# Who begins the 16 transfers that turn a state's last chunk into rows: SyncE and ScalarE, or SyncE alone

## What is computed

```python
for _ in range(5):
    a_in  = Af @ (state @ in_W.T + in_b)
    a_out = Af.T @ (state @ out_W.T + out_b)
    a = concat([a_in, a_out, state])
    r = sigmoid(a @ r_W.T + r_b);  z = sigmoid(a @ z_W.T + z_b)
    h_hat = tanh(concat([a_in, a_out, r * state]) @ h_W.T + h_b)
    state = (1 - z) * state + z * h_hat
out = layernorm(x + tanh(state @ o1_W.T + o1_b) @ o2_W.T + o2_b)
```

## Time and profile before

| | before |
|---|---|
| median of 3 runs | 664.33 us (664.10 to 664.61) |
| the profiled execution | 664.52 us |
| its span in the trace | 662.7 us |
| TensorE busy | 649.4 us, 98% |
| VectorE busy | 476.7 us, 72% |
| ScalarE busy | 409.9 us, 62% |
| GpSimd busy | 50.7 us, 8% |
| mean granted TensorE clock | 0.996 of full speed |

### The profile page before, as it was taken

The page is one execution under the profiler, slowest core; times in us unless marked ns, Lnnn a source line. Parts: engine busy times, 40 slices in busy tenths (PEclk is TensorE's granted clock), DMA queues, the critical chain, the costliest instruction groups (busy, mean ns, idle before and its releaser), DMA issues.

```text
span 662.7 us, 8655 instructions
## 1 busy us (share of the span) xinstructions
PE 649.4 (98%) x2940; PEld 538.7 (81%) x2940; DVE 476.7 (72%) x774; ACT 409.9 (62%) x550; POOL 50.7 (8%) x49
## 2 busy tenths in 40 slices
PE   8999999999999999999999999999999999999993
PEld 7888888888888888888888888888888888888883
DVE  4986878697487759847784994687489658725886
ACT  2873735479456837864593688368458935763646
POOL 0074034200400000000000000000000000000002
PEclk9999999999999999999999999999999999999998
DMA  8996533213000130300003022000322200013003
GB/s 286 311 407 241 169 130 106 42 42 52 3 0 32 51 47 32 52 13 0 32 33 62 0 64 32 0 32 32 50 46 60 35 1 1 1 64 127 1 1 130
DMA packets 90515, 46.72 MB, mean 70 GB/s; under 512 B 72176, under 2 KB 78960, under 8 KB 90224
## 3 DMA queue, kind: packets, MB, share of 16 engines
q1 hardware_dynamic: 86128, 45.77, 24.0%
q10 hardware_dynamic: 4352, 0.53, 0.5%
HBM read 32.12 MB, written 11.53 MB: 66 GB/s over the span
## 4 chain that ended last, share of the span: by engine, by line
PE 93%; DVE 3%; DMA 1%; SPq 1%; ACT 1%; issue 0%; DVEq 0%
PE bank L561 26%; PE bank L548 17%; PE bank L550 17%; PE bank L549 17%; PE bank L612 15%; DMA work<-in_x_dram 1%; DVE stats L1552 1%; DVE a L1545 0%; DVE sums L1524 0%; DVE ring L1139 0%; ACT rows L811 0%; SPq L389 0%; ACT a L1123 0%; SPq L391 0%; DVE work L1585 0%
## 5 line engine op out<-in xcount | busy, mean ns | idle before, releaser
L901 ACT ACTIVATE work<-work,bias 128x512 f32<-128x512 f32 x120 | 86.1, 723 | 155.5 <-DVE work L1280 155.0
L561 PE MATMUL bank<-ring,rows 128*128 128x512 f32 x768 | 178.6, 389 | 0.0
L561 PEld LDWEIGHTS bank<-ring,rows 128*128 128x128 f32 x768 | 144.0, 188 | 30.2 <-ACT ring L811 0.2
L1280 DVE SCALAR_TENSOR_TENSOR work<-degree,deg_w,bank 128x512 f32<-128x512 uint16 x120 | 88.7, 745 | 57.6 <-PE bank L550 56.5
L811 ACT ACTIVATE ring<-a 128x1024 fp32r<-128x1024 uint8 (+1 forms) x115 | 116.4, 1048 | 8.7 <-PE bank L561 6.6
L548 PE MATMUL bank<-u_c,fold 128*128 128x512 f32 x240 | 93.5, 389 | 0.0
L550 PE MATMUL bank<-u_c,fold 128*128 128x512 f32 x240 | 93.4, 389 | 0.0
L549 PE MATMUL bank<-u_c,fold 128*128 128x512 f32 x240 | 93.4, 389 | 0.0
L612 PE MATMUL bank<-ring,rows 128*128 128x512 f32 x256 | 65.0, 391 | 0.0
L548 PE MATMUL bank<-st_c,own 128*128 128x512 f32 x160 | 62.3, 389 | 0.0
L550 PE MATMUL bank<-st_c,own 128*128 128x512 f32 x160 | 62.2, 389 | 0.0
(11 more groups left out here) (147 smaller groups left out, 924.2 us busy)
## 6 DMA issues: line engine op xcount, KB each, us to landing
stage<-in_adj_dram SPq DMA_DIRECT2D x15, 512.0 KB, 8.9
sums<-in_adj_dram SPq DMA_DIRECT2D x13, 512.0 KB, 8.6
turned_dram<-work SPq DMA_DIRECT2D x12, 512.0 KB, 2.6
rows<-turned_dram SPq DMA_DIRECT2D x192, 32.0 KB, 2.0
work<-in_x_dram SPq DMA_DIRECT2D x4, 512.0 KB, 10.6
x_dram<-work SPq DMA_DIRECT2D x4, 512.0 KB, 8.8
a<-x_dram SPq DMA_DIRECT2D x4, 512.0 KB, 5.4
a<-in_adj_dram SPq DMA_DIRECT2D x3, 512.0 KB, 11.1
```

The source lines that it names most:

```text
L561: m = nc.tensor.matmul(u_bank[2 * (c % 2) + d][:, :], rows[:, part, j, d * P:(d + 1) * P], tile[:, jj, :], start=(first and jj == 0 and pa ...
L901: nc.scalar.activation(gates[:, g, e, :], gates[:, g, e, :], ACT.Tanh if g == H else ACT.Sigmoid, bias=bias[:, g, e:e + 1]).then_inc(gate_ ...
L1280: nc.vector.scalar_tensor_tensor(out=gates[:, g, e, :], in0=degree[:, c * CW:(c + 1) * CW], scalar=deg_w[:, g, e:e + 1], in1=g_bank[s % 3] ...
```

## The change

SyncE's `turn_move` runs over all four groups `n` and so begins 16 transfers. ScalarE's `turn_move` and its two calls for each step are gone. Sources, targets, sizes and the semaphore of the transfers stay as they are.

```diff
                 sp.wait_ge(turned, DB * NC * (t + 1))
-                for n in range(NQ - 1):
+                for n in range(NQ):
                     for r in range(NQ):
                         sp.dma_start(rows[n * SQ:(n + 1) * SQ, LO, ...
...
-            def turn_move(t, some):
-
-                k = NC - 1
-                act.wait_ge(turned, DB * NC * (t + 1))
-                for n in range(NQ - 1, NQ):
-                    for r in some:
-                        act.dma_start(rows[n * SQ:(n + 1) * SQ, LO, ...
...
                 for k in range(10, 12):
                     if side == 0:
                         row_high(t, 2, k - 10)
-                        turn_move(t - 1, range(2 * (k - 10), 2 * (k - 9)))
                     cast(t, side, k)
```

More of the change, by code:

```diff
@@ L867, in split_state @@
                 high(st_c[:, HI, e, :], stateT[:, e, c * CW:(c + 1) * CW], st_hi)
-            def turn_move(t, some):
-                k = NC - 1
-                act.wait_ge(turned, DB * NC * (t + 1))
-                for n in range(NQ - 1, NQ):
-                    for r in some:
-                        act.dma_start(rows[n * SQ:(n + 1) * SQ, LO, k * BC:(k + 1) * BC, :].bitcast(F32)
-                                      .rearrange("a b (e r d) -> a (b e) r d", e=DB, r=NQ)[:, :, r, :],
-                                      turned_T[r * SQ:(r + 1) * SQ, n].rearrange("p b e d -> p (b e) d")).then_inc(rows_loaded[k], 16)
             def row_high(t, k, h):
```

## The result

The changed kernel takes 666.91 us (median of 6 runs, 666.42 to 667.97), the kernel before 664.43 us (6 runs, 664.10 to 664.83). The ratio is 1.0038 with a 95% interval of 1.0026 to 1.0050: slower by about 2.5 us. Two more measurements of the same kernel, beside the experiments, gave ratios of 1.0034 (1.0021 to 1.0047) and 1.0033 (1.0021 to 1.0045). The profiled execution took 667.19 us, with a span of 665.4 against 662.7; the mean granted TensorE clock is 0.996 in both. One execution among the experiments, of the kernel with half-size transfers, took 942.8 us at a granted clock of 0.655 and is left out of its ratio.

A forecast was written before the change was run, and what follows sets the result against it. TensorE's own work was taken as the bound. 664.52 + 2.1 + 0.7 = 667.3 us for an execution like the profiled one, 0.2 less for the median: 667.1 us, 8-in-10 range 665.2 to 669.2.

The forecast's parts named there:

- TensorE bounds, nothing else gives: Whole kernel: TensorE is busy 98% of the span; changes elsewhere count only through its stream, and no later idle stretch returns delay.
- ScalarE's relief is worth 0: ScalarE: dropping its 16 issues, some 10 us of issuing, gains 0 because a lead of over 1 us hides them.
- Last issue 9.8 us after the first: SyncE's burst in each step: sixteen issues 0.652 us apart put the last start 9.8 us after the first.
- From the last issue to the row work, 1.98 us: Chunk 3 on ScalarE: `row_high` starts 1.96 to 1.99 us after SyncE's last issue starts; 1.98 enters the sum.
- The cast's end, 1.58 after that: ScalarE: the cast behind `row_high` ends 1.58 us after `row_high` starts, later than VectorE's low part at 1.36.
- 0.21 us from the cast's end to the load: TensorE at place 18: a weight load held up by a cast starts 0.21 us after the cast's end.
- 0.1 us absorbed: TensorE at place 18: loads run ahead of matmuls, so about 0.1 us of each late load is not lost.
- Clean losses of 0.50, 0.51, 0.51 and 0.62, together 2.1: TensorE, steps 1 to 4: time lost to the late first load of place 18, 2.1 us together.
- Hiccups: SyncE's bursts: stray extra issue time, 0.0115 us for each issue, now counts in full: 0.7 us for 64 issues.
- (a): Rival at place 18: the later transfers stay hidden if TensorE could stand 0.6 us more; 664.3 us, chance 0.09.
- (b): Rival: SyncE's interval falls once ScalarE stops issuing, below 0.62 us; time 664.3, at best 663.1 us; chance 0.05.
- (c): Rival: SyncE's interval stays 0.709 us, each step loses 1.35 us, 669.8 us; chance 0.11 including what lies beyond.

The follow-up runs named there:

- the one with the cast ahead: Against the changed kernel, ScalarE casts tiles 18 and 19 ahead of the high part of chunk 3's rows, not behind it: 665.75 us, ratio 1.0023.
- 14 and 2: Against the changed kernel, SyncE begins 14 of the 16 transfers and ScalarE the last 2, ahead of its cast 11: 664.33 us, ratio 1.0003.

## Why the prediction was right

The forecast was 667.1 us, the measurement 666.91, and the mechanism is the forecast one. By its steps:

- **TensorE bounds, nothing else gives.** Held: outside the four first sides the steady part changed by 0.01 us.
- **ScalarE's relief is worth 0.** Held, by the kernel that leaves four transfers out (0.9999). The kernel that adds four issues back on ScalarE came out 0.7 to 1 us slower than the changed one, with no late cast in its profile; whether the relief has a small worth once SyncE's chain is exposed stays open.
- **Last issue 9.8 us after the first.** Measured 9.78 to 9.84 in steps 2 to 4.
- **From the last issue to the row work, 1.98 us.** Measured 11.74 - 9.78 = 1.96. The cast's end, 1.58 after that, is exact.
- **0.21 us from the cast's end to the load.** Mis-sized: 0.13 (291.20 to 291.33). This makes the load 0.48 us late in step 2 and not 0.61. The row that the 0.21 was read from ends in "<-issue", so it did not show a load held up by a cast.
- **0.1 us absorbed.** Held, at its upper end: 0.48 late and 0.38 lost in step 2, 0.52 and 0.46, 0.58 and 0.52 in steps 3 and 4, so 0.06 to 0.10.
- **Clean losses of 0.50, 0.51, 0.51 and 0.62, together 2.1.** Measured 0.38, 0.46 and 0.52 in steps 2 to 4. Step 1 lost 1.56 with a last issue 10.93 us after the first in place of 9.8, so about 0.43 of it is the clean part: 1.8 in all, 0.3 too much forecast, mostly from the 0.08 us at the cast.
- **Hiccups, 0.7 us over 64 issues.** The size was near, 1.13 us in the profiled execution, 0.9 in the two others; the picture was wrong. They don't fall at random: one long interval stands in step 1's burst in each of the three profiles of the changed kernel, and steps 2 to 4 have none above 0.69. The forecast had 0.3 too much clean loss and 0.4 too little here, and the start and the end of the program, on which it was silent, took 0.24 off. Errors of 0.2 to 0.4 cancel, so that the agreement of 667.1 with 666.91 is closer than the terms deserve: that part is luck.
- **The rule of the Trainium skill** (DMA: Bandwidth & Descriptors, Issuing engines are not separate DMA queues) is that a second issuing engine saves only the time of initiating on the sequencer, "usually small relative to the DMA itself". Its first half agrees with the runs: SyncE took 10.4 us to issue all sixteen where its twelve had taken 7.9 to 8.4, and the median landing stayed at 2.0. Its "usually small" does not: one issue is a third of a landing here, and 16 in a row are five landings.

Of the rivals, (a), hidden anyway, is true of 14 transfers, of 15 where the burst is clean, and not of 16. For (b), SyncE's steady interval did not fall once it issued alone: 0.652. For (c), 0.709 on average was step 1's long interval and not a rate.

No version here beats the kernel before. The best with SyncE alone is the one with the cast ahead, at 665.75; 14 and 2 equals the kernel before.

## What to carry to other kernels

A burst of transfers of one shape costs its issuer nearly the same time for each (0.65 us here), and only the last one's landing counts: (number - 1) x interval + landing, set against the moment the data is wanted, tells how many one engine may begin. An idle engine is a good issuer only as long as that sum stays below the due time; the work hidden on a busy engine is free only up to its lead there. SyncE's edge came out of one profile to within one transfer; ScalarE's did not, where the loss beyond it was twice what the profile had suggested. When a late instruction names a releaser that ended well before it, look at what else it waits for: here moving that other work ahead gave back a third of the loss.

## What the runs showed of the hardware

Halving a transfer hardly changes the cost of its issue: 0.652 us for 32 KB in 8 pieces a partition, 0.643 for 16 KB in 4. The same shape with a DRAM source took 0.49.

One long interval among SyncE's issues stood in step 1 of every kernel, between 1.03 and 1.80 us; 1.65 and 1.40 us in two profiles of the same kernel. The DMA view of the kernel after, from 156.3 to 160.5 us, shows packets on two instruction queues in that stretch; from 277.8 to 282, in a clean burst, it shows none. From 156.3 to 160.5:

```profile
q1 hardware_dynamic: 803, 0.10, 15.6%
q8 instruction: 1, 0.02, 2.0%
q14 instruction: 1, 0.01, 0.8%
...
157.79 1.61 SPq L360 DMA_DIRECT2D rows<-work  x1
```

The issue that began at 157.79 took 1.61 us in place of 0.61, and the packet on queue 8 began at 157.62.

The DMA records of all 14 profiles say more. From 100 us on, each profile has two packets on queue 8 at SyncE's bursts, one near 158 us and one near 235 us, in a burst of line 376. In 27 of these 28 cases the packet overlaps the longest interval of the burst, of 1.03 to 1.80 us. The exception is step 1 of the kernel before: there the packet came at 156.26, ahead of the burst, and its one interval of 1.10 us has a packet on queue 14 in it, at 160.58. After 100 us no interval above 1.0 us in bursts of lines 360, 376 and 441 is without a packet on one of these two queues, and in the changed kernel the bursts of line 360 in steps 2 to 4 have neither such a packet nor a long interval.

This also tells why the place in the burst varies: the packet began at 157.62 in one profile of the changed kernel, and the third interval was long; it began at 158.78 in another, and the fifth was. So the two go together; which of them causes the other, and what the packet carries, no run shows. A packet on queue 14 alone mostly passes without a long interval, as at 159.90 in the kernel after.
